# Lower layer of a mixture of experts on one core: the pass loop run in five laps, with the second half of a tile's router logits behind the first pass

## What is computed

```
def kmoe(x_flat, W_router, A, B, scale, bias, d_in1, d_in2, d_out1, d_out2, top_k):
    logits = x_flat @ W_router.T
    vals, idx = jax.lax.top_k(logits, top_k)
    probs = jax.nn.softmax(vals, axis=-1)
    xs = x_flat.reshape(-1, d_in1, d_in2)
    Y = jnp.einsum('nkoi,nij,nkpj->nkop', A[idx], xs, B[idx])
    out = jnp.einsum('nkop,nk->nop', Y, probs).reshape(-1, d_out1 * d_out2)
    return out * scale + bias
h = kmoe(x_flat, W_up, A_up, B_up, scale_up, bias_up, 32, 32, 64, 64, 2)
h = jax.nn.gelu(h, approximate=False)
y = kmoe(h, W_down, A_down, B_down, scale_down, bias_down, 64, 64, 32, 32, 2)
```

## Time and profile before

| | us |
|---|---|
| median of 3 runs | 1376.31 (1376.28 to 1378.97) |
| profiled execution, its own time | 1373.84 |
| its span, first to last instruction | 1372.0 |
| upper layer, all tiles | 884 to 1150 |
| lower layer, tile 0 with the last tile's logits | 1151 to 1224 |
| lower layer, tiles 1 to 3 | 1224 to 1362 |

### The profile page before, as it was taken

How to read it: one execution, slowest core, us unless ns; L and a number is a source line. 1 busy time by engine, 2 the same in 40 slices (tenths; PEclk the granted TensorE clock), 3 DMA queues, 4 the chain that set the end, 5 groups by cost and what they waited for, 6 DMA issues and landing times.

```text
span 1372.0 us, 61950 instructions
## 1 busy us (share of the span) xinstructions
PE 1262.5 (92%) x27944; PEld 817.2 (60%) x27944; DVE 799.0 (58%) x1495; ACT 444.6 (32%) x927; POOL 227.8 (17%) x372
## 2 busy tenths in 40 slices
PE   6999999999999999999999997977888888898886
PEld 4865333333333334676666675666777777787775
DVE  2264776776777671556556553637273845357766
ACT  0222131122122112222122221336363636246554
POOL 0000000000000001222122220225152433113212
PEclk9999999999999999999999998989999999669998
DMA  6677889989989973411100111003330306513102
GB/s 257 217 243 198 283 292 306 308 276 318 300 279 319 292 282 88 77 61 61 61 31 31 61 46 62 32 2 153 92 123 31 122 0 246 213 66 128 82 36 92
DMA packets 68080, 211.50 MB, mean 154 GB/s; under 512 B 14448, under 2 KB 30832, under 8 KB 53520
## 3 DMA queue, kind: packets, MB, share of 16 engines
q1 hardware_dynamic: 67984, 210.16, 45.5%
HBM read 172.37 MB, written 37.75 MB: 153 GB/s over the span
## 4 chain that ended last, share of the span: by engine, by line
PE 76%; DVE 9%; issue 5%; DMA 4%; POOL 2%; SPq 1%; ACT 1%; DVEq 0%; POOLq 0%; ACTq 0%
PE ps L686 14%; PE ps L537 10%; PE ps L1058 8%; PE ps L2104 5%; DVE arena L549 4%; PE ps L234 4%; PE ps L1172 4%; PE ps L1079 4%; PE ps L2058 4%; PE ps L2073 3%; PE ps L444 3%; PE ps L2090 2%; PE ps L676 2%; PE ps L2037 2%; PE ps L2147 2%
## 5 line engine op out<-in xcount | busy, mean ns | idle before, releaser
L549 DVE STREAM_TRANSPOSE arena<-arena 128x448 f32<-128x448 f32 (+1 forms) x512 | 263.4, 577 | 100.1 <-PE ps L537 81.9
L537 PE MATMUL ps<-arena 32*64 32x400 f32 (+1 forms) x4096 | 202.5, 506 | 0.8
L686 PE MATMUL ps<-arena 128*64 128x512 f32 x832 | 189.2, 598 | 0.0
L537 PEld LDWEIGHTS ps<-arena 32*64 32x64 f32 x4096 | 75.0, 130 | 97.5 <-issue 50.2
L686 PEld LDWEIGHTS ps<-arena 128*64 128x64 f32 x832 | 55.6, 136 | 121.3 <-issue 111.9
L570 ACT ACTIVATE arena<-ps,arena 128x384 f32<-128x384 f32 x64 | 36.3, 582 | 276.4 <-DVE arena L561 276.4
L1971 ACT COPY arena<-ps 128x512 f32<-128x512 f32 x128 | 75.1, 587 | 144.2 <-PE ps L2073 81.1
L1058 PE MATMUL ps<-arena 128*128 128x256 f32 x512 | 115.3, 383 | 0.8 <-ACT arena L993 0.8
L1058 PEld LDWEIGHTS ps<-arena 128*128 128x128 f32 x512 | 97.3, 192 | 17.5 <-issue 3.3
L1800 DVE SCALAR_TENSOR_TENSOR arena<-ps,arena 128x512 f32<-128x512 f32 x64 | 68.9, 1104 | 37.7 <-PE ps L2090 37.5
L2104 PE MATMUL ps<-arena 64*64 64x32 f32 x4096 | 84.7, 236 | 6.3 <-DVE arena L1817 5.7
(11 more groups left out here) (144 smaller groups left out, 1859.5 us busy)
## 6 DMA issues: line engine op xcount, KB each, us to landing
arena<-ctx SPq DMA_DIRECT2D x64, 1024.0 KB
arena<-ctx SPq DMA_DIRECT2D x32, 768.0 KB
arena<-q_n SPq DMA_DIRECT2D x64, 256.0 KB, 11.3
h_n<-arena SPq DMA_DIRECT2D x16, 1024.0 KB, 4.5
arena<-h_n SPq DMA_DIRECT2D x16, 1024.0 KB, 9.5
arena<-x SPq DMA_DIRECT2D x16, 512.0 KB, 4.4
arena<-ctx SPq DMA_DIRECT2D x32, 256.0 KB
x_n<-arena SPq DMA_DIRECT2D x16, 512.0 KB, 3.5
```

The source lines that it names most:

```text
L537: last = pe.matmul(ps[b * SEQ:(b + 1) * SEQ, tb, 0:WIDTH[tb]], qs[p % 2][r, db, b * SEQ:(b + 1) * SEQ], z[r, at % RING, b, 0:WIDTH[tb]], s ...
L549: vec.transpose(z[:, at % RING, :, g * 224:g * 224 + nt * 32].rearrange("p b (j t) -> p b j t", t=32), slots[slot_of(k)][:, :, 0:nt, db * ...
L686: last = pe.matmul(ps[b * SEQ:(b + 1) * SEQ, OB, :], probt[:, j, b * SEQ:(b + 1) * SEQ], slot[:, b, jj, :], start=j == 0, stop=j == TILES - 1)
```

## The change

Three edits, all in the lower layer. PE's logits of the last tile are cut in two: 64 matmuls stay where they were, and 64 with the fold go behind the first pass of tile 0. For this the outer loop runs in five laps instead of four. Lap 0 has one pass (i = 0), lap 1 has six (i = 1 to 6), laps 2 to 4 have seven each (8 to 14, 16 to 22, 24 to 30), by the sums of `past`. What closed a lap before (two seconds, transposes, next gather) now stands under `If(lap > 0)`, and the second half of the logits under `If(lap < 1)`. PE's wait for `s_lge` is gone. DVE does `parts` and `logits` after `y_out` of step 1 instead of ahead of step 0. SP is the same.

```diff
@@ vector
-            if T == 0:
-                parts(T_N, 6)
-                logits(vec, "dn", T_N - 1, 6)
             for n in range(STEPS):
                 if n + 2 < STEPS:
                     stage_h(T, n + 2)
                 y_out(T, n)
+                if T == 0 and n == 1:
+                    parts(T_N, 6)
+                    logits(vec, "dn", T_N - 1, 6)
@@ tensor
-        def logits_dn(bank):
-            for p in range(F1):
+        def logits_dn(bank, part=range(F1)):
+            for p in part:
...
-            last.then_inc(s_lgd, 1)
+            if p == F1 - 1:
+                last.then_inc(s_lgd, 1)
@@
-        def steps_dn(T):
-            with pe.Fori(T * 8, T * 8 + 7) as i:
+        def steps_dn(lap):
+            past = [(lap + T_N - k) // T_N for k in range(1, T_N + 1)]
+            whole = past[2] + past[3]
+            with pe.Fori(past[0] + past[1] * 7 + whole * 8, past[0] * 6 + (past[1] + whole) * 8 + 1) as i:
                 second_dn(i * 2, 0)
                 first_dn(i * 2 + 2, 0)
                 second_dn(i * 2 + 1, 1)
                 first_dn(i * 2 + 3, 1)
-            second_dn(T * STEPS + STEPS - 2, 0)
-            second_dn(T * STEPS + STEPS - 1, 1)
@@
-        logits_dn(6)
-        fold_dn(T_N, 6)
-        pe.wait_ge(s_lge, 9)
-        with pe.Fori(0, T_N) as T:
-            steps_dn(T)
-            with pe.If(T < 1):
-                transpose_choices(pe, "dn", 6, T_N)
-                for e in range(2):
-                    pe.wait_ge(s_ohe["dn"][e], 4 + CREDIT)
-            with pe.If(T < T_N - 1):
-                pe.wait_ge(s_oc, T * 2 + 2)
-                gather_dn(T + 1)
+        logits_dn(6, range(F1 // 2))
+        with pe.Fori(0, T_N + 1) as lap:
+            steps_dn(lap)
+            with pe.If(lap < 1):
+                logits_dn(6, range(F1 // 2, F1))
+                fold_dn(T_N, 6)
+            with pe.If(lap > 0):
+                second_dn(lap * STEPS - 2, 0)
+                second_dn(lap * STEPS - 1, 1)
+                with pe.If(lap < 2):
+                    transpose_choices(pe, "dn", 6, T_N)
+                    for e in range(2):
+                        pe.wait_ge(s_ohe["dn"][e], 4 + CREDIT)
+                with pe.If(lap < T_N):
+                    pe.wait_ge(s_oc, lap * 2)
+                    gather_dn(lap)
```

## The result

| | before | changed |
|---|---|---|
| median of 12 runs, taken side by side, us | 1377.64 | 1391.30 |
| ratio changed / before, 95% interval | | 1.0076 (1.0041 to 1.0111) |
| profiled execution, us | 1373.84 | 1395.16 |
| its span, us | 1372.0 | 1393.4 |

By the ratio the change makes the kernel slower by 0.76%, about 10.5 us. The difference of the two medians is 13.7 us and that of the two means 9.1 us; the ratio lies between them and comes with an interval, so it stands for the result. The forecast was slower by 3.2 us, with a range up to 1391.

What follows compares the result with a forecast made beforehand. PE was taken to bound the kernel (busy 92% of the span). Second pass 2.0 us later plus 1.2 us for the laps made 3.2 us slower, 1376.31 + 3.2 = 1379.5 us; 8-in-10 range 1367 to 1391.

Steps and rivals of the forecast that it cites:

- The far jump of lap 0: Branch L2219 behind the fold skips 960 instructions to code not yet loaded; 5.5 us, bounds 3.5 and 6.4.
- half clock in six passes and the closing seconds: Tile 0 behind the jump: clock 0.50 as before, so passes 2 to 7 and closing seconds take the same 31 us.
- the stall that went: First pass of tile 0: 3.12 us stall, a code block arriving among the loads, which the change takes away.
- the rival with the lost order: Lap 0's jump brings all blocks in turn or throws out the loop's: +6 to +16 us; chance 0.15.
- The loads' share of the jump: Lap 0's jump behind the fold: its code block must pass the loads, 5.5 us against 3.5 in the quiet.
- The upper bound: Lap 0's jump: at most 6.4 us, from entering the loops at 1181.4 to PE going on at 1187.78 before.
- The first pass: Tile 0, between the logits' halves: 3.1 us at full clock plus 1.1 us for a new code block.
- the first pass at full clock: Tile 0's first pass, between the logits' halves, keeps full clock: 3.46 - 0.33 = 3.1 us.
- The laps: Laps 1 to 4: one more jump, untaken condition and register instructions each; 0.3 us a lap, 1.2 us in all.
- Cheap jump or clock held: Behind the fold: 3.5 us jump with clock held, -8 us, 1368; or code already there, 1365; chance 0.21.
- the lap no longer fits: Laps of 1,630 instructions, seven blocks, fetch code again each lap: +20 to +50 us, about 1410; chance 0.06.
- Nothing to measure: Jump behind the fold at 4 us, the laps' jumps hidden: 0 to +2 us, 1377; chance 0.08.

Runs made afterwards that it cites:

- a_late: Changed kernel with the loads of x2 and h held back until step 5 of tile 0 is through; 1381.96 us, ratio 1.0041.
- b_nowait: Kernel before without PE's wait for DVE's copy of the logits (s_lge) ahead of the loops; 1375.02 us, ratio 0.9986.
- a_fill: Changed kernel plus six dense matmuls that nobody reads, behind the fold in lap 0 ahead of the far jump; 1372.93 us, ratio 0.9963.
- a_laps: Changed kernel plus one dense matmul ahead of the last first_dn in every gather of the lower layer; 1385.88 us, ratio 1.0041.
- a_fill_late: Changed kernel with five dense matmuls behind the fold in lap 0 and the x2 and h loads held back until step 5; 1372.21 us, ratio 0.9958.
- b_fill5_late: Kernel before with five dense matmuls replacing the wait behind the fold, x2 and h loads held back until step 5; 1363.52 us, ratio 0.9900.
- b_bound: Kernel before with the inner loop's upper bound written as a sum of divisions, same value; one profile, 1383.8 us.
- a_swap: Changed kernel with its two conditions swapped: closing seconds, transposes and gather first, the logits' second half and fold last; 1386.19 us, ratio 1.0059.
- b_fill: Kernel before with six dense matmuls that nobody reads replacing PE's wait behind the fold; 1365.6 us, ratio 0.9927.
- b_fill_late: Kernel before with three dense matmuls replacing the wait behind the fold, x2 and h loads held back until step 5; 1369.53 us, ratio 0.9923.

## Why the prediction was right or wrong

**Direction and mechanism: right. The size: three times too small.** The far jump of lap 0 was the step on which all hung. It took 4.52 us (forecast 5.5, bounds 3.5 and 6.4), fell among the loads, and was followed by half clock in six passes and the closing seconds. No gain was left of the stall that went. But 10.5 us lie outside what the forecast gave by itself (-0.5 to +6 us). The stated range reaches that far only for the sake of the rival with the lost order (+6 to +16 us), which isn't what happened. That the range holds the ratio's 1376.31 x 1.0076 = 1386.8 us is therefore luck, and the median of 1391.30 stands at its very edge.

**The loads' share of the jump: mis-sized.** 2 us were taken, a_late against the changed kernel shows 1.06, other pairs 0.6 to 1.2. The upper bound was loose, since it dated the request for the block of before at the entry into the loops; b_nowait enters earlier, and the packet starts at the same time.

**The first pass: mis-sized, with a term missing.** The forecast gave it 1.1 us for the missed block; it was 1.56. What was not seen is that the clock would fall with this small stall, at 1181.4, in the middle of the pass. It did so in all five profiles with this stall (changed, a_fill, a_late, a_laps, a_fill_late). The length alone doesn't decide it: in the gather of the changed kernel PE stood for 1.56 us as well, up to 1168.84, and kept its clock. The `first_dn` behind the stall took 1.93 instead of 1.14 us, and the logits' second half 6.00 instead of 4.1. From the logits' start to the second pass the forecast had 19.8 us and the trace has 1196.04 - 1172.99 = 23.05: 3.25 more. These two are 2.7 of it, the stall 0.5, the first half of the logits 0.4 (4.15 for 3.78), the entry into the loops 0.3 (0.68 for 0.4), the rest of the pass 0.2, and the jump takes 0.8 off (5.29 us of standing still for 5.5 + 0.9 - 0.3). The step that failed is "the first pass at full clock".

**The laps: mis-sized.** The forecast had 1.2 us for jumps and conditions, 0.3 a lap, and didn't look at the pass's end. From the start of a tile's second pass to its closing seconds, tile 0 (at half clock) took 29.55 us before and 30.54 changed, tile 2 22.08 and 22.91, tile 3 21.56 and 22.55. In tile 1, where the changed kernel had the lower clock, a_fill_late against b_fill5_late gives 22.92 and 22.07. That makes some 3.7 us for 1.2. It comes in two parts. Most jumps back cost 0.10 us more, by the bound (b_bound), but where a pass waits for something else anyway (two passes a tile at full clock) nothing is seen of it. And the step from the last pass to the closing seconds takes 3.83 instead of 3.31 us: there the bound, the jump L2216 (215 ns) and the condition L2219 (79 ns) stand in a row. The bound was there to be read in the diff: it had become a sum of terms with divisions.

**Sum.** The forecast's 3.2, the 3.25 more up to the second pass (in which the cheaper jump is already counted), and 2.5 more for the laps make 9.0 us, against some 7.5 us (6.3 side by side) between those runs of either kernel that were not slowed by a further tile. The profiles give 1.6 us of it back. From the last pass of tile 0 to the next gather it takes 4.39 instead of 5.00 us. And from tile 0's first gather matmul to the logits it takes 19.62 instead of 20.61, because the trace of before had half clock there from 1169.4 to 1172.9 and the other had not, which the change doesn't explain. No further term is needed.

**The further tile at half clock: not in the forecast.** By the runs' clocks it came in 8 of 12 instead of one third (5 of 12 side by side, by the times), and that makes up the rest of the 10.5 us. The forecast treated the clock in tiles 1 to 3 as given because the one trace of before showed 1.00 there. The runs had been saying otherwise: their spread of 1376.28 to 1378.97 was small by luck of three, 12 runs of the same kernel spread over 15 us. Why the changed kernel falls more often is not settled. At the start of tile 1's passes it stood for 0.39 and 0.85 us, before for 0.44 and 0.42, but a_laps, made to test just that, didn't decide.

**The rivals.** "Cheap jump or clock held" fell: the least that a jump to code not yet run took in any profile is 3.3 us, and the clock fell. But its size was good: it stands 11.5 us under the forecast (1368 against 1379.5), and a_fill, where the clock held, took some 15.5 us off the changed kernel. At 0.9963 of before it still ends short of the 8 us that the rival gave. "Lost order of the instruction memory" and "the lap no longer fits" fell for the changed kernel: two more q8 packets, none in laps 2 to 4. But in a_swap a jump in lap 1 had to wait for code that lap 0 had run, so something like the first of them does happen. "Nothing to measure" fell.

## What to carry to other kernels

Ask of each jump over code that has not run yet whether its target is loaded, whatever the distance, and put the wait for it under work that is already queued. A condition that is skipped in the first lap makes such a jump, and a_swap shows one in the second lap. Where an engine with a clock of its own stands still ahead of thin work, work that nobody reads can be a cheap repair: 4.5 us of it, with the loads held back, made a tile 12 us shorter, and 5.4 us without that 11 us. And keep the bound of an inner loop a short expression, since it was worked out at every pass here.

## What the runs showed of the hardware that was not expected

A stall of 1.56 us on PE, in the middle of a pass, came with half clock in five profiles, and one of 3.80 us likewise; one of 1.56 us in the gather did not. In the lower layer full speed came back in or right behind the denser matmuls (logits, gather, transposes, filling), and in none of the 14 profiles in a tile's passes.

A far jump over 960 instructions costs no more than one over 514: 3.46 and 3.80 us (a_late, a_fill_late) against 3.52, which is 3.32 to 3.83 over the 14 profiles. So the blocks between don't seem to be fetched. With 5 MB of loads starting at the same time it takes 4.42, 4.52 and 4.68 us (a_fill, changed kernel, a_laps).

A lap of 1,630 instructions, once run, stays in PE's instruction memory: no q8 packet came after the gather of lap 1. Before that code can be lost: in a_swap the jump of lap 1 to the end of the outer loop, which lap 0 had run, took 2.99 us with q8 packets.

With matmuls of 128x128 by 128x512 that nobody reads the clock stayed at 1.00 through 4.5 to 5.4 us in which PE would have stood still, and in a_fill, b_fill, a_fill_late and b_fill5_late (five or six matmuls) no run of 42 had a mean clock under 0.963, where of the kernel before 33 of 104 had one under 0.962. With three (b_fill_late) one of 12 had 0.956.
